# A convolution, frequency-filter and token-MLP block on one core: token transposes in fp8, the first layer in fp16 on row tiles, another order on VectorE, and another order of the start

## The reference, cut to what matters

```
x = x + conv(ln_c(x))                # ln_c: over the 48 channels of each pixel
    # conv: 3x3 convolution of the first 12 channels, 1x1 to 254 channels,
    #       rfft2 of 8x8 patches, times a weight per channel and frequency, irfft2,
    #       gelu(first 127) * last 127, 1x1 back to 48 channels
t = tokens of x (one per pixel, 48 values)
t = t + ffn(ln_t(t))
    # ffn: h = relu(q_acc(q_acc(q(t) @ q(W1).T) + q(b1)))      48 -> 192
    #      y = q_acc(q_acc(q(h) @ q(W2).T) + q(b2))            192 -> 48
    # q rounds to fp8 (5 exponent, 2 mantissa bits), q_acc to fp16
```

## Time and profile before

| | |
|---|---|
| median of 3 runs | 804.11 us (802.82 to 804.41) |
| the profiled execution | 804.71 us, span of its trace 802.9 us |
| PE, weight loads, DVE, ACT, POOL busy | 88%, 65%, 78%, 63%, 71% of the span |
| granted TensorE clock | 0.98 of full speed on average |
| DMA | 76 GB/s over the span |
| chain that ended last | PE 63%, DVE 20%, issue 6%, POOL 3%, ACT 2%, DMA 1% |

### The profile page before, as it was taken

The page is one execution under the profiler, slowest core; times in us unless marked ns, Lnnn a source line. Parts: engine busy times, 40 slices in busy tenths (PEclk is TensorE's granted clock), DMA queues, the critical chain, the costliest instruction groups (busy, mean ns, idle before and its releaser), DMA issues.

```text
span 802.9 us, 20194 instructions
## 1 busy us (share of the span) xinstructions
PE 709.8 (88%) x6571; PEld 525.4 (65%) x6571; DVE 623.5 (78%) x1157; ACT 504.2 (63%) x962; POOL 571.7 (71%) x420
## 2 busy tenths in 40 slices
PE   1318999999999999989999999999999999999963
PEld 0206777777777667767777667777777766677731
DVE  5514788988888888888888888888888888877761
ACT  1203456767766676667777676767677766666674
POOL 2534578877887787877788778888778877854362
PEclk9998999999999999999999999999999999999995
DMA  3222323333333333323333233333333233232001
GB/s 65 44 60 72 77 75 96 68 89 93 91 86 78 75 95 96 95 66 96 91 91 84 68 87 96 95 96 68 89 92 91 76 82 81 76 91 57 20 20 40
DMA packets 46500, 62.35 MB, mean 78 GB/s; under 512 B 19039, under 2 KB 34871, under 8 KB 46391
## 3 DMA queue, kind: packets, MB, share of 16 engines
q1 hardware_dynamic: 46391, 61.00, 30.7%
HBM read 44.62 MB, written 16.35 MB: 76 GB/s over the span
## 4 chain that ended last, share of the span: by engine, by line
PE 63%; DVE 20%; issue 6%; POOL 3%; ACT 2%; DMA 1%; DVEq 1%; POOLq 0%; SPq 0%; ACTq 0%
PE inva L449 12%; PE invb L454 12%; PE mixp L436 12%; PE misc L497 5%; PE misc L463 4%; PE misc L536 4%; DVE gmix L808 4%; DVE st L873 3%; PE misc L482 3%; DVE zl L797 3%; DVE qpix L860 3%; PE misc L593 3%; PE misc L523 2%; PE misc L491 2%; DVE hbuf L819 2%
## 5 line engine op out<-in xcount | busy, mean ns | idle before, releaser
L808 DVE TENSOR_TENSOR gmix<-mixp,freq_w 128x508 f32<-128x508 f32 x256 | 163.7, 681 | 52.5 <-PE mixp L436 51.7
L645 ACT ACTIVATE hid<-misc 128x512 f16<-128x512 f32 x192 | 100.9, 598 | 78.2 <-PE misc L497 78.2
L436 PE MATMUL mixp<-win,zh 60*128 60x254 f16 x1024 | 120.7, 273 | 22.5 <-DVE zl L797 11.8
L449 PEld LDWEIGHTS inva<-inv,gmix 128*127 128x127 f32 x1024 | 129.1, 192 | 11.7 <-issue 2.1
L449 PE MATMUL inva<-inv,gmix 128*127 128x128 f32 x1024 | 135.9, 276 | 0.9 <-DVE gmix L808 0.9
L454 PE MATMUL invb<-inv,gmix 128*127 128x128 f32 x1024 | 135.2, 275 | 0.0
L454 PEld LDWEIGHTS invb<-inv,gmix 128*127 128x127 f32 x1024 | 124.6, 192 | 0.0
L436 PE MATMUL mixp<-win,zl 60*128 60x254 f16 x1024 | 119.4, 268 | 0.0
L654 ACT ACTIVATE hid<-hid 128x512 fp8e5<-128x512 f16 x192 | 106.2, 627 | 0.0
L971 POOL TENSOR_TENSOR ob<-tch,y 112x1024 f32<-112x1024 f32 x32 | 68.2, 2133 | 45.9 <-DVE y L882 45.9
L1014 POOL TENSOR_TENSOR st<-st,neg_half 128x16 f32<-128x16 f32 x32 | 92.9, 2903 | 10.8 <-DVE st L928 10.8
(11 more groups left out here) (103 smaller groups left out, 1261.0 us busy)
## 6 DMA issues: line engine op xcount, KB each, us to landing
xin<-in_x_dram SPq DMA_DIRECT2D x64, 192.0 KB, 3.5
xres<-in_x_dram SPq DMA_DIRECT2D x64, 192.0 KB, 4.2
out_dram<-ob SPq DMA_DIRECT2D x64, 192.0 KB, 3.6
taps<-cz_scratch SPq DMA_DIRECT2D x32, 292.5 KB
crm<-rm_scratch SPq DMA_DIRECT2D x64, 96.0 KB
cz_scratch<-cz SPq DMA_DIRECT2D x64, 48.8 KB
cx<-in_x_dram SPq DMA_DIRECT2D x32, 96.0 KB
rm_scratch<-rm_t SPq DMA_DIRECT2D x128, 4.0 KB
```

What stands on the lines that cost most here:

```text
L436: mm = pe.matmul(mixp[q][:, e * HID2:(e + 1) * HID2], zpart[r0:r0 + KC, 2 * s + e, :], win[r0:r0 + KC, wpart, :], start=(e == 0 and zpart ...
L449: mm = pe.matmul(inva[0:HID, q * PX:(q + 1) * PX], gmix[:, s % 2, q, 0:HID], inv[:], start=True, stop=True, skip_group_check=True)
L645: act.activation(hid16[:, 3 * c + g, :], bank[banks[g]][:], ACT.Copy).then_inc(hid16_ready, 1)
L808: dve.tensor_tensor(gmix[:, s % 2, 2 * q:2 * q + 2, 0:HID2], mixp[q][:, 0:2 * HID2].rearrange("p (e c) -> p e c", e=2), freq_w[:], ALU.mul ...
```

## The change

1. `qpix` is written as fp8 by VectorE; the eight token transposes become matmuls with an fp8 identity `eye8` as the moving operand, 128 columns of weights. ScalarE copies the result out as fp16 (`q16`), which changes no value.
2. The first layer's weights are copied once to fp16 (`l1h`), and g = 0 reads only partitions 0 to 47, g = 1 only 64 to 111 (before, all 112, with zeros in the weights). In the second group both wait for both banks ahead of g = 0.
3. On VectorE the bias of y and the first weighing stand ahead of the sum of the squares of x.
4. The start: x(1) is loaded ahead of the constants; the pads are written from ScalarE's queue; the biases are loaded later under a semaphore of their own; in steps 0 and 1 SyncE sends the rows right behind the x load; the first row transposition comes after the transposes of x(1); in step 2 GpSimd makes cz before the power; ScalarE copies the rows ahead of the next reordering of x.

```diff
@@ SyncE
             load_cx((0, 0), 0)
-
+            sp.wait_ge(x_zeroed, 2)
+            load_x((0, 0), -1)
             sp.dma_start(raw_fft[:], ...
...
+                if early:
+                    if a == 0:
+                        setup()
+                    rows_out(t)
+                    if a == 0:
+                        biases()
                 if live(t, 0) and not (isinstance(a, int) and a == 0):
                     sp.wait_ge(cmul, upto(a))
                     sp.sem_inc(sp_held, 1)
                     load_cx(t, 0)
+                if early:
+                    rows_in(t)
@@ TensorE
             def hidden(t, c, g, dst):
-                pe.sem_inc(pe_held, 1)
-                pe.matmul(dst[:], l1[0:SPAN, g, :], q8[:, 4 * c:4 * c + 4, :], start=True, stop=True,
+                r0, r1 = ((0, CH), (HALF, SPAN), (0, SPAN))[g]
+                pe.matmul(dst[:], l1h[r0:r1, g, :], q16[r0:r1, 4 * c:4 * c + 4, :], start=True, stop=True,
...
+                    pe.sem_inc(pe_held, 1)
                     for i in range(PAIRS):
-                        mm = pe.transpose(bank[i // 4][0:SPAN, (i % 4) * PX:(i % 4 + 1) * PX],
-                                          qpix[:, i, 0:SPAN], eye[:])
+                        mm = pe.matmul(bank[i // 4][:, (i % 4) * PX:(i % 4 + 1) * PX], qpix[:, i, :], eye8[:],
+                                       start=True, stop=True, skip_group_check=True)
...
                     pe.wait_ge(hid16_ready, upto(6 * k + 2))
+                    pe.wait_ge(hid16_ready, upto(6 * k + 3))
                     hidden(t, 1, 0, bank[0])
-                    pe.wait_ge(hid16_ready, upto(6 * k + 3))
@@ ScalarE
+            act.wait_ge(row_zeroed, 1)
+            for part in range(2):
+                for r in (0, PR - 1):
+                    images = cz_d[part].rearrange("c (b r) w -> c b r w", b=BATCH)
+                    act.dma_start(images[:, :, r, :], zero_row[0:CC, :].unsqueeze(1).to_broadcast([CC, BATCH, PW]))\
+                      .then_inc(pads_out, 16)
             order_x((0, 0), 0)
@@ VectorE
-            dve.memset(xin[:, 0, :], 0.0).then_inc(set_dve, 1)
-            dve.memset(xin[:, 1, :], 0.0).then_inc(set_dve, 1)
-            dve.wait_ge(set_dve, 4)
-            dve.sem_inc(x_zeroed, 1)
+            dve.memset(zero_row[:], 0.0).then_inc(row_zeroed, 1)
+            for half in range(2):
+                dve.memset(xin[:, half, :], 0.0).then_inc(x_zeroed, 1)
...
+                    dve.sem_inc(dve_held, 1)
-                    dve.tensor_tensor(halves(qpix)[:, :, 0:CH], tcen[:], rstd, ALU.mult)\
+                    dve.tensor_tensor(halves(qpix)[:, :, 0:CH], tcen[:], rstd, ALU.mult, saturate=False)\
...
+                if live(t, 6):
+                    dve.wait_ge(y16_ready, upto(2 * l + 2))
+                    dve.tensor_scalar(y16[:], y16[:], bq[0:SPAN, 2:3], None, ALU.add).then_inc(yb_ready, 1)
+                if live(t, 3):
+                    weigh(t, 0)
                 if live(t, 0):
                     dve.wait_ge(xsq_ready, upto(a + 1))
                     dve.tensor_reduce(st1[:, 1, :], xsq[:], AX_X, ALU.add).then_inc(stat1, 1)
@@ GpSimd
-                filling = isinstance(t[0], int) and t[1] < 3
+                filling = isinstance(t[0], int) and t[1] < 2
```

More of the change, by code:

```diff
@@ L107, in metaformer_kernel @@
         l1 = sb("l1", [128, 3, 128], F8)
+        l1h = sb("l1h", [128, 3, 128], F16)
+        eye8 = sb("eye8", [128, 128], F8)
         l2 = sb("l2", [128, 3, 128], F8)
@@ L337, in setup @@
                         sp.dma_start(raw_b[HALF * j:HALF * j + CH, 2:3],
[L338 to L343, removed]
@@ L346, in step, with rows_in @@
+            def rows_in(t):
+                a = at(t, 0)
+                sp.wait_ge(rm_out, upto(64 * (a + 1)))
+                sp.wait_ge(csub, upto(a))
+                sp.sem_inc(sp_held, 1)
+                for kind in range(2):
+                    src = rm_d[ring(t, 0), kind].rearrange("(g q) w -> g (q w)", g=CG)
+                    sp.dma_start(crm[:, kind, :], src.unsqueeze(0).to_broadcast([CC, CG, 2 * W]))\
+                      .then_inc(rm_in, 16)
             def step(t):
                 a, n, m, k, l = (at(t, d) for d in (0, 3, 4, 5, 6))
-                if live(t, -1):
+                early = isinstance(t[0], int) and t[1] < 2
+                if live(t, -1) and not (isinstance(t[0], int) and t[1] == 0):
@@ L526, in step @@
                             mm.then_inc(xT_done, 1)
+                    if peeled and a == 1:
+                        rows(t, 1)
                 if live(t, 3):
@@ L692, in step @@
                                        bank[1 + q][0:SPAN, :], ACT.Copy).then_inc(y16_ready, 1)
+                if filling and t[1] == 1:
+                    rows(t, 1)
+                if filling and t[1] > 0:
+                    rows(t, 0)
                 if live(t, -1):
@@ L834, in residual, with rows @@
                                   ALU.add).then_inc(tch_ready, 1)
+            def rows(t, behind):
+                a = at(t, behind)
+                dve.wait_ge(pow1, upto(a + 1))
+                dve.wait_ge(rmT_done, upto(a))
+                order = lambda i: st1s[:, ring(t, behind), i, :].rearrange("p (i j) -> p j i", j=2)
+                dve.tensor_tensor(rm[:, 1], order(6), order(2), ALU.mult).then_inc(mr_ready, 1)
             def relu(t, c):
@@ L866, in step @@
                     dve.tensor_scalar(st1[:, 2, :], st1[:, 0, :], 1.0 / CH, None, ALU.mult).then_inc(mean1, 1)
+                if isinstance(a, int) and a == 1:
+                    rows(t, 1)
                 if live(t, 3):
@@ L899, in step @@
                     weigh(t, 2)
-                if live(t, 0):
-                    dve.wait_ge(pow1, upto(a + 1))
-                    dve.wait_ge(rmT_done, upto(a))
-                    order = lambda i: st1[:, i, :].rearrange("p (i j) -> p j i", j=2)
-                    dve.tensor_tensor(rm[:, 1], order(6), order(2), ALU.mult).then_inc(mr_ready, 1)
+                if live(t, 0) and not (isinstance(a, int) and a == 0):
+                    rows(t, 0)
                 if live(t, 4):
```

128 lines of the change are left out of this document (68 added, 60 removed).

## The result

The changed kernel takes 769.71 us in the median of 4 runs (767.5 to 771.26), the kernel before 803.83 beside it: a ratio of 0.9576, 95% interval 0.9559 to 0.9593. The profiled execution took 770.88 us, span 768.9, at a mean granted clock of 0.98.

A forecast was written before the change was run, and what follows sets the result against it. TensorE's queue was taken to set most of the 22.21 us step. Start 11, 27 steps of 0.85 (23) and end 1.5 sum to 35.5: 804.71 becomes 769.2, less 0.6 gives 768.6 us; range 757 to 781.

The forecast's parts named there:

- The start, 11 us: Before the first convolution matmul: reordered loads and rows bring it from 57.37 to 46.1, taken as 11 us; bounds 7 to 12.5.
- Eight token transposes in 0.68: TensorE's token transposes in fp8 take 0.68 us instead of 0.91, saving 0.23 a step; bounds 0.46 to 0.91.
- the hole of 0.28: TensorE's wait for the weighing ahead of the second mixing; claimed gone, moving that mixing 0.54 earlier, transposes included.
- Row tiles, 0.31: First layer's matmuls on TensorE: pairs run side by side, saving 0.10 in the first group and 0.21 in the second.
- The drain of the rival: TensorE tiling-mode switches: if each drain cost a whole matmul, row tiles would be worth 0.02 and the time 776.
- The hole of 0.34 stays: TensorE's wait ahead of the first mixing stays, since the reduction and the product of 2.02 before it are untouched.
- the second loop: Third weighing through GpSimd's power and normalising product to first mixing: 22.0 of 22.21 us, slack 0.2, shrinking to 21.36.
- Power behind the output addition, nothing lost: GpSimd's power, ready at about 380.9 against 381.22 today, still follows the output addition, which also comes earlier; nothing lost.
- The steps of the end: Steps 32 and 33, TensorE alone, gain 0.54 each; the last three gain 0.4 in all: 1.5 us.
- fp8 type of qpix and the extra semaphore step, nothing: VectorE writing qpix as fp8 after one more semaphore step costs nothing; if it showed, under 0.1 a step.
- The rival of half steps: Steps give 12 us instead of 23, through tiling drains or a longer GpSimd loop: 779.5 us; chance 0.15.
- The rival of slower, a late y: ScalarE delivers y late, so VectorE's bias holds its queue and the second mixing; 823 us at 2 us wait; chance 0.03.

The follow-up runs named there:

- steps_only: Kernel before plus changed token transposes, row tiles and VectorE order (parts 1, 2, 3), with the old start: 781.29 us, ratio 0.9708.
- order_only: Kernel before plus only the new VectorE order (y's bias and first weighing ahead of the sum of squares): 797.01 us, ratio 0.9897.
- full_rows: Changed kernel with the first layer's fp16 matmuls on all 112 rows instead of row tiles: 782.37 us, ratio 0.9716.
- turn_fp32: Changed kernel with the token transposes in fp32 as before, without the extra semaphore steps for fp8: 781.28 us, ratio 0.9708.
- zpix_residual: Changed kernel with the first residual ahead of VectorE's sum of squares and GpSimd's `zpix` directly behind `xcen`: 767.58 us, ratio 0.9519.

## Why the prediction was right

The time was 769.7 against 768.6. Its steps one by one:

- **The start, 11 us.** Measured 10.89 in the trace and 10.7 by `steps_only`. Every stage came within 0.7 us: xpix(1) ended at 18.58 (18.5), the fetch was issued at 25.29 (24.7), cz(0) started at 28.91 (28.6), xpix(2) ended at 34.52 (34.3), cz(1) directly behind xsq(2) ended at 39.16 (38.6), and the convolution started at 46.48 (46.1), 7.32 after it. The copy of the weights to fp16 took 3.05 us, not a part of half a microsecond, and lay in the cover that I named.
- **Eight token transposes in 0.68: mis-sized.** They take 0.56 with the switch, 0.45 without it: 56 ns each, the lower end of my bounds, nothing but the pass. From the first to the second mixing are 2.54 us in place of 3.35, 0.81 less where I had 0.54: the transposes gave 0.22 more than I took, and the hole of 0.28 was worth 0.34 from start to start, as `order_only` shows (1.02 from the first transpose to the second mixing, before 1.36).
- **Row tiles, 0.31.** On TensorE they save that: 0.11 for the first group and 0.22 for the second. The drain of the rival (the Trainium skill, TensorEngine Tiling (Array Packing), Key Properties) is not seen as a whole matmul: the price of a switch stays the 0.11 of the rows.
- **The hole of 0.34 stays: wrong.** It is 0.56. I argued that the sum of x and the product in front of it are untouched, and read the product's 2.02 as its length. It is 0.81 behind GpSimd's squares, and they are behind the power: the hole was already the meeting of TensorE with the second loop. That loop had no slack of 0.2: the 22.0 of my sum lacks the 0.22 between the power's end and the product's start, which belongs to it, since the mixing follows the power's end by 3.65 and not the product's start by 3.43. With that it is the whole period, and 22.21 less 0.81 and 0.11, plus the first layer's 0.18, is the 21.47 measured. So of the row tiles' second group, 0.21 in my sum, nothing remains.
- **Power behind the output addition, nothing lost: half right.** The power of x starts 0.53 after that addition, behind the small operations, and yet 4.07 after the first mixing where it was 4.28. What I didn't list as late next is the residual behind the sum of squares: it delays the first layer by 0.14 and 0.21 in turn.
- **The sum.** 0.81, 0.11 and 0.22 gained, 0.22 and 0.18 lost: 0.74 a step, as by the period, against 0.85 predicted. The steps of the end run in 20.04 in place of 20.57, 0.53 each (0.54). Steps and end together gave 23.1, predicted 24.5; since the median lies 1.2 below the profiled run here and lay 0.6 below it in the sum, part of that came back.
- **fp8 type of qpix and the extra semaphore step, nothing.** Right: the product ends 0.81 after GpSimd's squares with both of them (`full_rows`) and without (`turn_fp32`, before).
- **Slips of the working.** 376.94 + 1.04 + 1.01 + 1.02 - 0.23 is 379.78, and the text goes on with 379.75, so its 0.54 should be 0.51, 0.8 us in all. And 154 us are 6.93 steps of 22.21, not 7: a step held 19.1 us of VectorE and 17.9 of GpSimd, not 18.9 and 17.7. Neither moves a conclusion.

The rival of half steps named the loop over GpSimd. It binds, but at 21.47 a step. The rival of slower, a late y, didn't occur: VectorE's bias waits 0.2 us in all over seven steps.

So the forecast was close partly by luck: two errors cancel, a second mixing that came 0.27 earlier than I took and two waits of 0.40 together that I left out. That the order and the transposes need each other was shown (14.5 against 23.4 us). That the tokens' power holds the first mixing was shown by one move of GpSimd's `zpix`, which brought the power forward and took the hole away. That the row tiles' second group falls into the hole is read from 0.34 and 0.56 in kernels without and with them; a run with row tiles in one group alone was not made.

## What to carry to other kernels

A short wait in front of an engine that seems to set the pace is a loop that ties with it: follow it back to its first releaser before calling it fixed, and price an edit by whether it lies inside that loop. Where several loops tie, an edit that opens one of them only finds the next. An edit that shortens the work ahead of an existing wait is worth nothing until the wait's releaser moves, so test such parts together as well as one by one. Before moving an operation of VectorE or GpSimd, look at what it will then run beside on the other engine.

## What the runs showed of the hardware

**VectorE and GpSimd hold each other up.** L980, a small operation, takes 1.08 us beside `zpix` and ends 0.02 after it. With `zpix` moved it takes 0.18. Two relus of 0.74 together take 1.97 beside `tcen`, and the normalising product ends 0.81 after GpSimd's squares in every kernel, be it 1.14, 1.69 or 2.10 long. L980 in the stretch from 190 to 344 us, in the changed kernel and in `zpix_residual` (busy us, mean ns, idle before):

```profile
L980 DVE SCALAR_TENSOR_TENSOR st<-st 128x16 f32<-128x16 f32 x7 | 7.5, 1078 | 0.2
```

```profile
L980 DVE SCALAR_TENSOR_TENSOR st<-st 128x16 f32<-128x16 f32 x7 | 1.2, 176 | 0.2
```

The Trainium skill, SBUF — State Buffer, section Who interferes with whom, says that the two engines share a pair of ports as a lock for a whole instruction, with the later one standing still, for a VectorE operation in a two-port mode or with two SBUF inputs. The traces agree: the operations named here end a fixed time after GpSimd's, 0.81 for the product, 0.15 for the relus, 0.02 for L980. That 0.02 is less than the 0.18 that L980 takes alone, so the record does not show it standing still up to GpSimd's recorded end.

**In fp8, new weights for every 128 columns cost next to nothing here.** The eight transposes take 0.56 with the switch of 0.11, so 56 ns each, against 53 for a quarter of the 0.213 us that the prediction has for 512 columns. The Trainium skill, TensorE: Matmul & The Clock Gate, section Back-to-back issue gap, gives some 81 ns for such pairs; an estimate by that page is 0.65 for the eight and 0.26 saved. The measurement decides: 0.45.
